# Moving last stores, copies, shares and expert outputs between the stages of a two-layer kernel

## What is computed

```
xn = layernorm(x)                                   # layer 0
s  = attention(xn)            # 16 heads of 16, rotary keys and queries, softmax over 2048 keys
logits = xn @ gate_w.T + gate_b; probs = softmax over the 2048 rows
vals, idx = top 8 rows of each of 32 experts, per sequence
merged = sum_k vals[k] * xn[idx[k]]                 # one row for each sequence and expert
o   = gelu([merged, 1] @ w1[e]) ; o = [o, 1] @ w2[e]
ffn = zeros; ffn[idx] += o * vals
x   = x + s * silu(ffn)
# layer 1: x = x + scan_block(layernorm(x)) * silu(gated_mlp(layernorm(x)))
```

## Time and profile before

| what | us |
|---|---|
| median of 3 runs | 2851.25 |
| lowest and highest | 2848.01 and 2854.64 |
| the profiled execution's own time | 2858.88 |
| its span | 2857.10 |
| prepare, about | 0 to 285 |
| attention, about | 285 to 843 |
| scatter, about | 843 to 893 |
| layer 1, about | 893 to 2857 |

### The profile page before, as it was taken

How to read it: one execution, slowest core, us unless ns; L and a number is a source line. 1 busy time by engine, 2 the same in 40 slices (tenths; PEclk the granted TensorE clock), 3 DMA queues, 4 the chain that set the end, 5 groups by cost and what they waited for, 6 DMA issues and landing times. The chain is left out here.

```text
span 2857.1 us, 37061 instructions
## 1 busy us (share of the span) xinstructions
PE 2544.6 (89%) x13290; PEld 1481.0 (52%) x13290; DVE 2307.1 (81%) x2865; ACT 2024.1 (71%) x3261; POOL 2058.5 (72%) x680
## 2 busy tenths in 40 slices
PE   6886779999967699999999999999999999999978
PEld 2443233444424356656566565665655656656555
DVE  6675567777823598998989989899899898998985
ACT  3322356666643697887878879788798797988864
POOL 0556101111121699999999999999999999999996
PEclk9998789999988799999999999999999999999989
DMA  6247959999532321313213123032130321312210
GB/s 180 94 132 190 284 131 235 219 234 241 162 110 70 126 104 38 127 46 111 104 38 127 63 93 125 17 127 88 68 127 29 118 99 53 126 41 109 105 37 8
DMA packets 129488, 323.84 MB, mean 113 GB/s; under 512 B 15741, under 2 KB 84349, under 8 KB 112782
## 3 DMA queue, kind: packets, MB, share of 16 engines
q1 hardware_dynamic: 107034, 249.05, 28.4%
q0 software_dynamic: 19968, 71.38, 8.1%
q10 hardware_dynamic: 2304, 1.05, 0.2%
HBM read 286.75 MB, written 43.13 MB: 115 GB/s over the span
## 5 line engine op out<-in xcount | busy, mean ns | idle before, releaser
L1474 DVE TENSOR_TENSOR_SCAN l_st<-l_p_a,l_hl,l_st 128x512 f32<-128x512 f32 x768 | 932.4, 1265 | 106.8 <-ACT l_p_a L1733 97.7
L1655 POOL TENSOR_TENSOR l_st<-l_st,l_cs 128x2048 f32<-128x2048 f32 x192 | 871.0, 4560 | 0.0
L1733 ACT ACTIVATE l_p_a<-l_dt,lw_a_neg 128x512 f32<-128x512 f32 x1024 | 664.6, 680 | 44.9 <-DVE keep_xg L1474 36.9
L1647 POOL TENSOR_TENSOR l_st<-l_bs,l_dtu 128x2048 f32<-128x2048 f32 x128 | 583.7, 4560 | 32.1 <-PE l_p_y L2004 29.8
L2004 PEld LDWEIGHTS l_p_y<-keep_ident,l_st 128*128 128x128 f32 x3072 | 358.6, 146 | 141.9 <-POOL l_st L1655 72.9
L2004 PE MATMUL l_p_y<-keep_ident,l_st 128*128 128x128 f32 x3072 | 388.1, 283 | 45.4 <-POOL l_st L1655 45.2
L989 ACT ACTIVATE a_pr<-a_p_s 128x512 f32<-128x512 f32 x512 | 284.9, 596 | 168.7 <-PE a_p_s L1052 164.9
L903 DVE TENSOR_REDUCE a_mpart<-a_p_m 128x1 f32<-128x512 f32 x512 | 311.4, 681 | 8.9 <-PE a_p_m L1014 8.0
L1474 DVE TENSOR_TENSOR_SCAN keep_xg<-l_p_a,l_hl,keep_xg 128x512 f32<-128x512 f32 x256 | 314.7, 1266 | 1.9 <-issue 0.4
L1655 POOL TENSOR_TENSOR keep_xg<-keep_xg,l_cs 128x2048 f32<-128x2048 f32 x64 | 292.5, 4570 | 2.0 <-ACT l_hl L1738 2.0
L835 POOL DMA_DIRECT2D a_w<-in_w_dram x32 | 23.1, 725 | 351.0 <-PE a_p_m L1080 294.3
(11 more groups left out here) (232 smaller groups left out, 3961.5 us busy)
## 6 DMA issues: line engine op xcount, KB each, us to landing
l_bs<-s_bc SPq DMA_DIRECT2D x64, 1024.0 KB, 4.7
l_cs<-s_bc SPq DMA_DIRECT2D x64, 1024.0 KB, 4.8
a_w<-in_w_dram POOLq DMA_DIRECT2D x32, 1024.0 KB, 11.9
late<-in_w_dram POOLq DMA_DIRECT2D x32, 1024.0 KB, 19.2
kx<-s_kp SPq DMA_DIRECT2D x96, 256.0 KB, 12.7
keep_share<-s_x SPq DMA_DIRECT2D x32, 512.0 KB, 4.9
s_kp<-late SPq DMA_DIRECT2D x96, 128.0 KB, 2.1
s_vp<-late SPq DMA_DIRECT2D x16, 544.0 KB, 3.3
```

What stands on the lines that cost most here:

```text
L1474: eng.tensor_tensor_scan(st[k % NG][:, n, :], p_a[:, n, :], st[k % NG][:, n, :], hl[:, k, n:n + 1], ALU.mult, ALU.add).then_inc(scan_ok, 1)
L1647: eng.tensor_tensor(st[n][:, :, :], bs[:, 4 * n:4 * n + 4, :], dtu[(k // NG) % 2][:, :].unsqueeze(1).broadcast_to([P, NG, TT]), ALU.mult). ...
L1655: eng.tensor_tensor(st[n][:, :, :], st[n][:, :, :], cs[:, 4 * n:4 * n + 4, :], ALU.mult).then_inc(cm_ok, 1)
L1733: eng.activation(p_a[:, n, :], dt[c % 2][:, :], ACT.Exp, scale=a_neg[:, c, m:m + 1]).then_inc(dA_ok, 1)
```

## The change

It touches the borders between the first three stages and leaves layer 1 alone.

- The last two `keys_out` (tiles 14 and 15, 14 DMAs) leave the prepare stage and stand in the attention's `load(1)`. `group_queries` comes right behind `keys_out(13)`. ACT's two `store_queries` come one tile earlier.
- The copies of x leave `load` and follow it as `copy_x(i)`, which wait for chunk 96 + 4i: two for each of the last four `weigh`.
- `one_choice` runs four steps later than before, its last four behind the last `maxima`. DVE's first bias addition waits for `b1` alone (16), and step 4 for the three other loads.
- POOL issues the second `w1` before the first `w2`, and stores the outputs of quad 6 before it loads the last `w2`.
- `outputs(6)` moves from chunk 1 of `weigh(15)` to chunk 4 of `weigh(14)`, with `experts_out(6)` in the middle of the last `maxima`. `outputs(7)` moves from chunk 3 of `weigh(15)` to chunk 5. The last `hidden_rows` waits for one more store.
- Scatter loads the experts' outputs first, then `w_o`; `b_o` counts on `wo_in`, for which PE waits; DVE does `heads(0)` before the sum `oeb`.

```diff
-                for t in range(NT + 2):
+                for t in range(NT):
                     if t >= 2:
                         keys_out(t - 2)
...
-                    if t == NT:
-                        group_queries()
+                group_queries()
                 eng.wait_ge(side, 16 * (1 + 2 * 7 + 2 * 6))
...
-                    if t in (13, 14):
-                        store_queries(eng, t - 12)
+                    if t in (12, 13):
+                        store_queries(eng, t - 11)
...
+                def keys_out(r):
+                    p = r % 3
+                    for g in range(6):
+                        eng.dma_start(...[r, g // 2, g % 2], kp[p][:, g // 2, g % 2, :]).then_inc(stored[p], 16)
+                    eng.dma_start(..., vo[p][:, :, :]).then_inc(stored[p], 16)
...
                     if g == HG - 1:
+                        eng.wait_ge(consts, 16)
...
-                    if hg % 2:
-                        half = bass.ds(b * S + hg // 2 * (S // 2), S // 2)
-                        eng.dma_start(scr["x1"][half, :]...).then_inc(x1_out, 16)
+                    if g == 1:
+                        keys_out(NT - 2)
+                        keys_out(NT - 1)
+
+                def copy_x(i):
+                    eng.wait_ge(pv_ok, 8 * 12 + 4 * i)
+                    part = bass.ds(i * (S // 2), S // 2)
+                    eng.dma_start(scr["x1"][part, :]...).then_inc(x1_out, 16)
...
                 load_first(0)
+                load_first(1)
                 load_second(0)
-                load_first(1)
                 for q in range(1, QUADS):
                     if q + 1 < QUADS:
                         load_first(q + 1)
+                    else:
+                        store(q - 1)
                     load_second(q)
-                    store(q - 1)
+                    if q + 1 < QUADS:
+                        store(q - 1)
...
+                        if i == 26 and g == G - 1:
+                            experts_out(QUADS - 2)
...
                         if g == 1:
-                            eng.wait_ge(consts, 16 * 4)
+                            eng.wait_ge(consts, 16)
...
-                    one_choice(*prev(g, b, hg))
+                    if g == HG:
+                        eng.wait_ge(consts, 16 * 4)
+                    if g >= HG:
+                        one_choice(g - HG, b - 1, hg)
                     take(*prev(g, b, hg))
...
-                    wait(eng, eo_out, (q - 1) * 64)
+                    wait(eng, eo_out, (q if q == QUADS - 1 else q - 1) * 64)
...
-                            if c == 1 and hh == 1 and hg % 2 and g > 1:
+                            if c == 1 and hh == 1 and hg % 2 and 1 < g < G - 1:
                                 outputs(b * QB + hg // 2 - 1)
...
-                        if c == 3 and g == G - 1:
+                        if c == 4 and g == G - 2:
+                            outputs(QUADS - 2)
+                        if c == 5 and g == G - 1:
                             outputs(QUADS - 1)
...
+                eng.dma_start(oe[:, :], scr["oe"]...).then_inc(oe_in, 16)
                 eng.dma_start(w_o[:, :, :], ins["Wo"]...).then_inc(wo_in, 16)
-                eng.dma_start(oe[:, :], scr["oe"]...).then_inc(oe_in, 16)
...
-                eng.dma_start(b_o[:, :], ins["b_o"]...).then_inc(oe_in, 16)
+                eng.dma_start(b_o[:, :], ins["b_o"]...).then_inc(wo_in, 16)
...
-                eng.wait_ge(wo_in, 16)
+                eng.wait_ge(wo_in, 32)
```

More of the change, by code:

```diff
@@ L739, in attention_stage @@
         identb = sb("identb", [P, P], BF16)
+        kp = [late[:, j * 3 * TT:(j + 1) * 3 * TT].bitcast(BF16).rearrange("p (c e t) -> p c e t", c=3, e=2) for j in range(3)]
+        VN = HG * 4 * 4 * VW
+        vo = [late[:, 9 * TT + j * VN:9 * TT + (j + 1) * VN].rearrange("p (a n) -> p a n", a=HG) for j in range(3)]
         kst = [k[0:RM, :].bitcast(BF16).rearrange("p (c z t) -> p c z t", c=NC, z=4) for k in kx[1:] + kx[:1]]
@@ L821, in load @@
                             eng.dma_start(dst, src).then_inc(consts, 16)
-                    if hg % 2:
-                        half = bass.ds(b * S + hg // 2 * (S // 2), S // 2)
-                        eng.dma_start(scr["x1"][half, :].rearrange("(p a) d -> p (a d)", p=P),
-                                      ins["x"][half, :].rearrange("(p a) d -> p (a d)", p=P)).then_inc(x1_out, 16)
+                    if g == 1:
[4 more added lines that the diff above has]
+                    part = bass.ds(i * (S // 2), S // 2)
+                    eng.dma_start(scr["x1"][part, :].rearrange("(p a) d -> p (a d)", p=P),
+                                  ins["x"][part, :].rearrange("(p a) d -> p (a d)", p=P)).then_inc(x1_out, 16)
                 passes(eng, load)
+                for i in range(2 * B):
+                    copy_x(i)
                 eng.wait_ge(x1_out, 16 * 2 * B)
@@ L947, in step @@
                         return
-                    one_choice(*prev(g, b, hg))
+                    if g == HG:
+                        eng.wait_ge(consts, 16 * 4)
+                    if g >= HG:
+                        one_choice(g - HG, b - 1, hg)
                     take(*prev(g, b, hg))
                 def last():
-                    one_choice(G - 1, B - 1, HG - 1)
+                    for hg in range(HG):
+                        one_choice(G - HG + hg, B - 1, hg)
                     place()
-                    experts_out(QUADS - 2)
                     experts_out(QUADS - 1)
@@ L1020, in transpose_max @@
                     eng.wait_ge(np_ok, g + 1)
-                    wait(eng, eo_ok, (g - 2) // 2)
+                    wait(eng, eo_ok, QUADS - 1 if g == G - 1 else (g - 2) // 2)
                     for zm in range(8):
@@ L1150, in _ @@
             def _(eng):
+                eng.dma_start(oe[:, :], scr["oe"].rearrange("b e n -> (b e) n")).then_inc(oe_in, 16)
                 eng.dma_start(w_o[:, :, :], ins["Wo"].rearrange("(k p) m -> p k m", p=P)).then_inc(wo_in, 16)
-                eng.dma_start(oe[:, :], scr["oe"].rearrange("b e n -> (b e) n")).then_inc(oe_in, 16)
                 for b in range(B):
                     eng.dma_start(b2[b * NE:(b + 1) * NE, :], ins["b2"]).then_inc(oe_in, 16)
-                eng.dma_start(b_o[:, :], ins["b_o"].partition_broadcast(P)).then_inc(oe_in, 16)
+                eng.dma_start(b_o[:, :], ins["b_o"].partition_broadcast(P)).then_inc(wo_in, 16)
                 for dst, src in ((fc1[:, :, :], ins["fc1_w"]), (in_t[:, :, :], ins["in_projT"])):
@@ L1172, in _ @@
             def _(eng):
-                eng.wait_ge(oe_in, 16 * (2 + B))
-                eng.tensor_tensor(oeb[:, :], oe[:, :], b2[:, :], ALU.add).then_inc(oeb_ok, 1)
                 def heads(k):
@@ L1201, in _ @@
                         heads(k)
+                    if k == 0:
+                        eng.wait_ge(oe_in, 16 * (1 + B))
+                        eng.tensor_tensor(oeb[:, :], oe[:, :], b2[:, :], ALU.add).then_inc(oeb_ok, 1)
+                    if k == 1:
+                        eng.wait_ge(wo_in, 32)
                     if k:
```

4 lines of the change are left out of this document (added).

## The result

The changed kernel takes 2822.05 us (median of 4 runs, 2819.68 to 2827.5) against 2850.93 us before (4 runs), a ratio of 0.9892 with a 95% interval of 0.988 to 0.9904. That is 28.9 us less, where 41.6 were forecast: the gain is 12.7 us short. The time lies inside the range, near its upper end, and 12.4 us above the forecast of 2809.6 (the kernel before had four runs now instead of three, which moves its median by 0.3). In a later set the changed kernel was timed again, beside other kernels: 2823.68 us against 2854.28, ratio 0.9893.

The account below looks back on a forecast made before the run. Three stalls ahead of an unchanged layer 1 were to be won: border 9.4, step 1 24.9, shares 1.0, last outputs 6.3, scatter 0, together 41.6 us. From 2851.25 this gave 2809.6 us; 8-in-10 range 2802 to 2824.

Parts of the forecast that it names:

- Border: Between prepare and attention: with stores moved and query loads earlier, attention starts at 276.0 instead of 285.4, gaining 9.4 us.
- step 1: Attention's step 1: DVE no longer waits for the rank load, so 53.2 us falls to 28.3, gaining 24.9 us.
- last outputs: End of attention: 9.9 us back from the stall at `outputs(7)`, 3.6 us lost to `outputs(6)` in `weigh(14)`; gain 6.3 us.
- the shares: `one_choice` between maxima, twelve instead of fifteen: 1.0 us gained in step 3, nothing separately in the other steps.
- Step 3: Attention's step 3, which loses its `one_choice` between maxima: gain of 1.0 us, bounds 0 and 1.4.
- the step at 427.83: The step two after step 1 in the old trace, 30.93 us long, taken as the model for step 1.
- the held border: Rival at prepare's end: DMA engines hold the query loads, so none of the 9.4 us is won; 2819 us, chance 0.15.
- Scatter: Stage after attention: PE itself waits for `b_o`, then does four more transposes; counted 0, bounds -0.3 and +1 us.
- The releaser: Rival in step 1: keys or weights hold PE, not the rank load, so 22.8 us stay; 2832 us, chance 0.05.
- the late store: Rival near attention's end: quad 6's store lands late before `hidden_rows(7)`, costing 14 us; 2824 us, chance 0.07.
- the copies: Rival on the slower side: eight copies of x do not fit into the last four steps; 2872 us, chance 0.03.
- The stores' work: Rival early in attention: the moved key stores make something late there by 8 us; 2818 us, chance 0.09.

Follow-up runs that it names:

- kernel 5: The changed kernel with the key stores of tiles 14 and 15 issued by prepare again and ACT's query stores a tile later: 2827.61 us, ratio 0.9909.
- 6: The changed kernel with `outputs(6)`, `outputs(7)` and quad 6's store placed as before the change: 2825.49 us, ratio 0.9906.
- 9: The kernel before with one edit, the three rank loads issued by the first step instead of the fourth: 2831.76 us, ratio 0.9922.
- the repeat: The changed kernel itself, unaltered, timed and profiled again in a later set: 2823.68 us, ratio 0.9893.
- kernel 10: The changed kernel with the copies of x issued by the loads of the odd steps again: 2821.99 us, ratio 0.9888.
- kernel 2: The changed kernel with the two kinds of `one_choice` exchanged within each pair of steps: 2815.97 us, ratio 0.9867.
- Kernel 7: The changed kernel with odd steps' `one_choice` before the `turned` wait, `outputs(6)` back in `weigh(15)` chunk 1, `outputs(7)` in chunk 6, `b_o` first: 2804.58 us, ratio 0.9825.
- 8: Kernel 7 with `b_o` back in its place and the copies of x three chunks apart instead of four: 2799.03 us, ratio 0.9811.

## Why the prediction was right, and where it was 12.7 us off

**The mechanisms held.** Border, step 1 and last outputs were forecast at 40.6 us and measured at 36.0 between the first profiles. Kernels 5, 6 and 9 undo or do each alone and give 5 to 7 us, 1.3 to 5.2 us (4 by the ratios) and 22 us.

**The term whose sign was wrong: the shares.** The step was "Twelve `one_choice` instead of fifteen run between maxima. In odd steps each keeps PE waiting, 1.20 us". I counted choices and did not look at which. Before, an odd step ran the choice of the step before it, of even `hg`, the short kind (3.2 us on DVE); four steps back has the same `hg`, so now it runs the long one (3.67). Two things follow. At full clock a step takes 29.06 us with no choice there, 30.93 with a gap of 1.20 and 31.39 with one of 1.67: 0.46 us for each of five steps, 2.3 us. The rest of the 9.5, 7.2 us, is the clock: fallen in five of these steps instead of two, by 1.5 to 2.5 us each. In the repeat the four steps 5 to 11 lost 3.1 us instead of 6.6, and `weigh(13)` 0.5 instead of 2.9. That a clock can fall there stood in the trace of before, in the two odd steps of 0.95; I had not looked at the clock by step.

**Step 3** gave 1.9 us where I allowed 1.4 at most. This was the same fact in small: a choice behind the bias addition costs 1.9 us (30.93 - 29.06), not 1.2, as PE goes on waiting for maxima in small pieces after the gap (0.21 us of it shows as a wait). Seen in time, it says that all odd steps had 1.9 us to win by moving the choice rather than shifting it.

**Step 1** was forecast at 28.3 us and takes 28.32 at full clock (the repeat), but the exact hit is luck. The sum took the step at 427.83 and subtracted 2.66 us for `outputs`; that step also held a choice, which step 1 no longer has, and the sum said that this gain was in the term without subtracting it. Measured, the choice is worth 1.87 us (30.93 against 29.06 in step 3) and the work that step 1 lacks 0.74 (29.06 against 28.32): 2.61 together, beside the 2.66 put down to `outputs` alone. ACT's wait of 2.66 us was not what `outputs` cost the step.

In the first profile the clock of step 1 fell to 0.94, which is the missing 1.5 us. PE stops there for 2.71 us, for ACT, in all eleven traces in which step 1 has neither `outputs` nor a choice, and the clock fell in five of the eleven. Four of these five had a shorter step 0, 56.7 to 56.9 us, while the six that did not fall had 58.0 to 58.2: the clock, at 0.50 for the first 28 us of the stage, rose sooner (0.82 against 0.52 in kernel 10, from 28 to 32 us). Both steps together took 86.3 to 86.8 us in ten of the eleven, and 89.4 in kernel 2. So step 0's gain of 1.3 us in the table and step 1's missing 1.5 belong together; why they come as a pair stays open.

**The border** came at 276.99 against my 276.0, by two errors that nearly cancel, so this is luck in part too. The query loads were issued by 268.7 and not by 274, as the queue did not push back; then the stage's end came at 277.0, 8.3 us later, where I had allowed 5. That it is their landing which ends the wait is inferred; if so, the rival of the held border came true in part. My 9.4 was also taken from one execution in which prepare ended late: POOL's last addition lies between 266.6 and 269.6 in the traces. Taken from POOL's end it is 7.2.

**The last outputs**: + 3.6 for `outputs(6)` is exact (31.02 to 34.63). The stall gave 9.0 us and not 9.9 in the first profile and 6.4 in the repeat, since I let the clock stay at 2.4 GHz throughout. I counted 0 for taking `outputs(6)` out of the place beside the gelu; without it PE idled 3.14 us there and came back at 0.50, for one to four chunks of `weigh(15)`. Where it stands there again (kernels 7 and 8), the clock stays at 1.00. So this term was 0.9 us too high at best and 3.5 in the repeat, about as much as the odd steps lost there.

**Scatter** took 49.8 us in both, as forecast, though PE's wait for `b_o` is 8.0 us now; in the repeat it took 51.7. Kernel 7 shows the gathered rows as the next wait.

**The rivals.** The releaser, the late store (issued by 768.8, before the load, and landed in 1.6 us) and the copies did not come: SP's last copy was issued by 799.5, and the DMA share was down to 0.03 in 805 to 810, ahead of the stage's end at 812.7. A copy's median landing was 6.1 us, and that of the last four 5.5. The Trainium skill, "DMA: Bandwidth & Descriptors", section "Anatomy of one DMA — SWDGE (gpsimd) path", gave an estimate of 4.4; its figures are for DMAs that POOL issues, and SP issues these. The stores' work did not come back (kernel 5). None of my rivals was the loss in the odd steps or the one in `weigh(15)`. The held border gave 2819 and the late store 2824, but the measured 2822 comes near them in number only.

**The sum** was made against one execution and carried to the median. The two profiles differ by 31.4 us and the medians by 28.9; the 2.5 between them lie within what executions of either kernel differ by. The profiled execution of before is on the long side in work that the change does not touch: POOL ended prepare's arithmetic at 271.7, and in the twelve other traces at 268.5 to 271.4; layer 1 took 1963.8 us, and 1960.0 to 1963.2 in the others. The repeat's span is 36.3 us below it, and 5.6 of these lie in prepare and layer 1.

## What to carry to other kernels

When work is shifted by some steps of a loop, list which variant of it lands in which step, on the engine whose next instruction is waited for. A small job of an engine that idles later in the same step belongs into that idle time; here this was worth more (16 us) than fine placement elsewhere. Read the granted clock step by step before pricing a gap of TensorE: the gap's own length can be the smaller part of its price. And profile the same kernel twice before an account is drawn up from one trace: two rows of the table above moved by 6.0 and 2.6 us.

## What the runs showed of the hardware that I had not expected

Gaps of PE of about 1 us and more, at the head of a step of 30 us in otherwise dense work, were followed by a fall of its granted clock to the lower level, in 1 of 2 cases at 0.97 us, 6 of 17 at 1.20 and 18 of 25 at 1.67, and in none at 0.81 or below (0 of 23, those without a gap among them). A fall cost 1.1 to 2.5 us. Length is not all: in step 1 a stop of 2.71 us was followed by a fall in only 5 of 11 traces, and step 5 fell in all nine traces in which its gap was 0.98 us or more. After the stop of 3.14 us in `weigh(15)` the clock fell in all of eight traces, for one to four chunks of `values`, and `weigh(15)` took 1.3 us more for each further chunk. The Trainium skill, "TensorE: Matmul & The Clock Gate", section "A second HAM failure mode: psum-queue depth-cycling", tells of short stops between groups of matmuls that let the clock go to and fro; these traces agree (18 of 25 steps with a stop of 1.67 us). What else decides, at equal gaps, no run here shows.
